# A GraphSAGE stack: edge rows of the late steps gathered by indirect DMA, layer-norm moments of three chunks on the scalar engine, the last chunk of the last layer in halves

## The chip, the cores and the metric

One core of one Trainium2 chip runs the whole program in one launch. The metric is the device time in microseconds. Engines are named PE (TensorE), DVE (VectorE), ACT (ScalarE), POOL (GpSimd) and SP (SyncE, which here only issues transfers).

## The reference

```python
h = maximum(layernorm(x), 0)          # x: 3125 x 256, no gain or bias
src, dst = edge_index                 # 50000 edges, sorted by dst
def sage(x, Wl, Wr, b):
    agg = segment_sum(x[src], dst)    # 3125 nodes
    deg = segment_sum(1, dst)
    return (agg / maximum(deg, 1)) @ Wl + x @ Wr + b
h = relu(sage(h, Wl1, Wr1, b1))       # 256 -> 256
h = relu(sage(h, Wl2, Wr2, b2))       # 256 -> 128
h = relu(sage(h, Wl3, Wr3, b3))       # 128 -> 256
out = x + sage(h, Wl4, Wr4, b4)       # 256 -> 256
```

## The kernel before

**The sum over edges as matmuls.** The kernel builds a dense matrix `counts` (source by destination, f16) and keeps it for all four layers. Destinations go in seven chunks: six of 512 (`CH`) and one of 53. They are worked in `ORDER = [5, 6, 4, 3, 2, 1, 0]`; "q=0" is the first of them, chunk 5. The aggregate of a chunk is, for each of 25 tiles k of sources (`NT`), four matmuls of 128x128 by 512 columns: two halves `h` of the features by two f16 `parts` (a high and a low part, `H[..., 0, :]` and `H[..., 1, :]`) of the features (`add_sources`, L1925). Then DVE scales by 1/degree (`scale_agg`, L1354), and PE applies the weights in f32 (`lin`: L1841 in layer 1, L1865 in layer 4).

**How counts is made.** Edges are cut into 892 "steps" of 128 edges, each for a window of four or eight destinations. Of each step DVE makes two one-hot tables with `is_equal` (`step`, L1261; a group of three or four steps in two instructions, three groups in flight), PE multiplies them into `window_ps` (L1776), and ACT copies each pair of windows, once done, into `counts` (L1546). `window_ps` has two banks, so PE is at most two pairs ahead of the copies. The steps are in `PIECES` of 64, 115, 358 and 355. The first 64 are made ahead of q=0 (call this stage -1), the next 115 (36 pairs of windows) inside q=0 from k=5 on, the others in q=2 to q=5. `script(q)` writes out the order of sums, steps and linear parts, and every engine follows the same script; `first_round`, at "sum k" of q=0, says what else DVE and ACT do at each k. The queues are in order, so an item in `first_round` delays everything behind it on its engine.

**The tables of the steps.** A step's 128 edges lie in the rows `src16` and `dst16` (98 partitions of 608 edges, row overlapping row). Where a step begins comes from the rank of its window (`lo`), by `bases`; `base_late` holds it in units of 32 edges. For pieces 2 and 3, `choose_late` (DVE, L1075) compares the bases with the number of each of 16 groups: 16 instructions of 98x358 for each piece. At k=13 and k=19 of q=0 (`SELECT_K`) PE fetches the edges with them: `select_rows` (L1707) is 16 matmuls for the sources and 16 for the destinations, each 98x128 by 358 columns. From the result ACT (`late_sources`, k=14 and 20; `spread_sources`, k=18 and 23) and DVE (`late_tables`, k=16 and 22) make `step_src` and `step_key`.

**Layer norm.** For place j of `ORDER`: `h0_moments(j)` on DVE (four `bn_stats`, L1014, four `bn_aggr`, L1017), `h0_root` on ACT (L1502), `h0_shift` on DVE, `h0_relu` on ACT (one instruction a tile, L1511), `h0_high_part` on ACT (L1518), `h0_low_part` on DVE (L1033). Moments of places 4, 5 and 6 are at k=1, 8 and 12 of q=0. PE's sums of q=0 go through the tiles in the order of the places: place 4's tiles from k=12, 5's from k=16, 6's from k=20.

**The end of layer 4.** Chunks alternate between the banks `agg_ps` and `window_ps`. The last chunk's 98 matmuls come with the linear part of the chunk before it at k=4; then two scalings (L1354), `lin(4, NCH - 1)` (16 f32 products, two records each, in groups of two tiles), two additions (`add_out`, L1456) and one store of 512 KB (L762).

## Time and profile before

| | us |
|---|---|
| median of 3 runs (lowest to highest) | 698.95 (697.97 to 699.79) |
| the profiled execution | 696.64 |
| its span | 694.9 |
| stage -1, ends about | 45.2 |
| q=0, from k=5 to its last sum | 58.3 to 107.6 |
| last chunk of layer 4, from its first matmul | 654.0 |

Busy time in the profiled execution: PE 647.0 us (93% of the span), DVE 307.6, ACT 170.1, POOL 33.3. An engine's busy time over the whole span is an average of very different stages: DVE is busy 90% of the time at first and hardly at all in the last layers. In the timeline each row merges instructions of a kind; its bracket is idle time of the engine just ahead and who ended it. A row of the table of stretches has the stretch, its length, the busy time (and number of instructions) of PE, PE's weight loads, DVE, ACT and POOL, the granted share of TensorE's full clock, the busy share of the DMA engines, and GB/s.

### The profile page before, as it was taken

Reading aid. Unit: us, or ns where it says so; the run is one execution under the profiler, and the core shown is the slowest. Engines: PE = TensorE matmul, PEld = TensorE weight load, DVE = VectorE, ACT = ScalarE, POOL = GpSimd, SP = SyncE. Lnnn points to the kernel's source line nnn. Section 1 sums busy time; section 2 is a strip of 40 time slices with the busy share of each in tenths; the row PEclk is TensorE's granted clock in tenths of the full one; section 3 lists DMA queues with packets and bytes.
Section 4 is the critical chain, followed back from the end, with each engine's and each line's share of the span. In section 5 each row is a group of like instructions: output and inputs, shape, how many; then the busy total and the mean of one; then the engine's idle time right before and its main releaser. Section 6 shows DMA issues by size and latency. Waiting matters only on the chain.

```text
span 694.9 us, 10754 instructions
## 1 busy us (share of the span) xinstructions
PE 647.0 (93%) x4179; PEld 350.3 (50%) x4180; DVE 307.6 (44%) x846; ACT 170.1 (24%) x335; POOL 33.3 (5%) x86
## 2 busy tenths in 40 slices
PE   5568898899999989999999999999999999999996
PEld 4234555665554545545444444544445646546554
DVE  6889876478897888932122222222221110101001
ACT  4844663264542631310011010211220000000000
POOL 7000000000000000000000000000001020110110
PEclk9999998899999999999999999999999999999999
DMA  8100020410100101013133122211131123032130
GB/s 253 42 3 3 15 81 2 173 36 5 44 22 20 62 18 64 1 21 125 57 130 108 60 75 92 64 65 61 60 98 69 38 80 107 1 106 63 43 106 31
DMA packets 33431, 43.49 MB, mean 63 GB/s; under 512 B 6031, under 2 KB 18851, under 8 KB 33385
## 3 DMA queue, kind: packets, MB, share of 16 engines
q1 hardware_dynamic: 33268, 42.62, 19.1%
q8 instruction: 31, 0.51, 0.3%
q10 hardware_dynamic: 116, 0.24, 0.1%
q14 instruction: 16, 0.12, 0.1%
HBM read 26.73 MB, written 15.79 MB: 61 GB/s over the span
## 4 chain that ended last, share of the span: by engine, by line
PE 84%; DVE 10%; ACT 3%; issue 2%; POOL 1%; DVEq 0%; POOLq 0%; ACTq 0%
PE agg_ps L1925 31%; PE window_ps L1925 21%; PE lin_ps L1841 7%; PE lin_ps L1865 6%; PE window_ps L1776 6%; PE lin_ps L1882 5%; DVE early L1261 4%; PE turn_ps L1907 2%; ACT counts L1546 1%; PE lin_ps L1890 1%; PE lin_ps L1947 1%; DVE rdeg L1339 1%; DVE aggT L1354 1%; PE degree_ps L1707 1%; PE turn_ps L1707 1%
## 5 line engine op out<-in xcount | busy, mean ns | idle before, releaser
L1925 PE MATMUL agg_ps<-counts,H 128*128 128x512 f16 (+3 forms) x1026 | 235.1, 355 | 5.9 <-DVE aggT L1354 5.9
L1261 DVE TENSOR_TENSOR early<-early 128x512 f16<-128x512 bf16 (+2 forms) x466 | 151.8, 390 | 26.1 <-PE window_ps L1776 25.0
L1546 ACT ACTIVATE counts<-window_ps 128x400 f16<-128x400 f32 x196 | 96.4, 504 | 127.1 <-PE window_ps L1776 123.2
L1776 PEld LDWEIGHTS window_ps<-early 128*128 128x128 f16 x892 | 68.8, 100 | 112.9 <-ACT counts L1546 31.8
L1776 PE MATMUL window_ps<-early 128*128 128x100 f16 (+1 forms) x892 | 100.5, 222 | 23.9 <-DVE early L1261 13.5
L1925 PEld LDWEIGHTS agg_ps<-counts,H 128*128 128x128 f16 (+1 forms) x1026 | 80.2, 98 | 61.3 <-issue 14.6
L1925 PE MATMUL window_ps<-counts,early 128*128 128x512 f16 (+2 forms) x396 | 89.0, 379 | 0.0
L1925 PE MATMUL window_ps<-counts,H 128*128 (+3 forms) x339 | 66.6, 351 | 0.0
L1925 PEld LDWEIGHTS window_ps<-counts,early 128*128 128x128 f16 (+1 forms) x396 | 38.4, 98 | 46.7 <-issue 3.4
L1925 PE MATMUL agg_ps<-counts,early 128*128 (+3 forms) x297 | 46.9, 314 | 0.0
L1925 PEld LDWEIGHTS window_ps<-counts,H 128*128 128x128 f16 (+1 forms) x339 | 29.4, 98 | 33.8 <-issue 1.5
L1354 DVE SCALAR_TENSOR_TENSOR aggT<-agg_ps,columns,rdeg 128x512 f32<-128x512 f32 (+1 forms) x27 | 17.0, 659 | 63.0 <-PE agg_ps L1925 56.6
L1354 DVE SCALAR_TENSOR_TENSOR aggT<-window_ps,columns,rdeg 128x512 f32<-128x512 f32 (+1 forms) x15 | 10.4, 716 | 67.1 <-PE window_ps L1925 64.7
L1587 ACT ACTIVATE newT<-lin_ps,columns 128x512 f32<-128x512 f32 (+1 forms) x28 | 17.3, 632 | 89.9 <-PE lin_ps L1882 57.3
L1362 DVE SCALAR_TENSOR_TENSOR partsT<-newT,columns,partsT 128x512 f16<-128x512 f32 (+1 forms) x21 | 14.4, 684 | 52.9 <-ACT partsT L1602 52.1
L1456 DVE TENSOR_TENSOR newT<-lin_ps,newH 128x512 f32<-128x512 f32 (+1 forms) x13 | 8.7, 671 | 58.3 <-PE lin_ps L1865 54.1
L943 POOL TENSOR_TENSOR newH<-newH,plan 128x256 f32<-128x256 f32 (+1 forms) x25 | 17.3, 723 | 356.7 <-DMA newH<-in_x_dram 356.7
L1925 PEld LDWEIGHTS agg_ps<-counts,early 128*128 128x128 f16 (+1 forms) x297 | 22.0, 97 | 23.8 <-issue 1.1
L1841 PE MATMUL lin_ps<-aggT,W 128*128 128x512 f32 (+1 forms) x56 | 27.6, 600 | 0.7 <-DVE aggT L1354 0.7
L1865 PE MATMUL lin_ps<-W,aggT 128*128 128x256 f32 (+1 forms) x100 | 25.8, 380 | 1.3 <-DVE aggT L1354 1.3
L1865 PE MATMUL lin_ps<-W,selfT 128*128 128x256 f32 (+1 forms) x100 | 25.7, 379 | 0.0
L1841 PE MATMUL lin_ps<-selfT,W 128*128 128x512 f32 (+1 forms) x56 | 25.6, 562 | 0.0
(185 smaller groups left out, 452.7 us busy)
## 6 DMA issues: line engine op xcount, KB each, us to landing
selfT<-hT_d SPq DMA_DIRECT2D x18, 512.0 KB, 4.3
hT_d<-newT SPq DMA_DIRECT2D x12, 512.0 KB, 4.3
rdeg<-rdeg_d SPq DMA_DIRECT2D x18, 256.0 KB, 4.3
counts<-in_x_dram SPq DMA_DIRECT2D x6, 512.0 KB, 8.0
hT_d<-counts SPq DMA_DIRECT2D x6, 512.0 KB, 3.2
newH<-in_x_dram SPq DMA_DIRECT2D x6, 512.0 KB
out_dram<-newT SPq DMA_DIRECT2D x6, 512.0 KB
hT_d<-newT SPq DMA_DIRECT2D x6, 256.0 KB, 4.0
```

What stands on the lines that cost most here:

```text
L943: nc.gpsimd.tensor_tensor(x4[0:q, i, :], x4[0:q, i, :], b4rows[0:q, :], ALU.add).then_inc(x4_biased, 1)
L1261: last = v.tensor_tensor(hot[:, group % GROUPS, 0:n * size].rearrange("p (r n d) -> p r n d", r=n, d=2), numbers_to[:, 0:size].rearrange(" ...
L1354: v.scalar_tensor_tensor(out=aggT[:, h, 0:n], in0=(agg_ps, window_ps)[bank][:, h, 0:n], scalar=unscale[:, l - 1:l], in1=rdeg[:, 0:n], op0= ...
L1362: v.scalar_tensor_tensor(out=low, in0=(lin_ps if l == 1 else newT)[:, h, 0:n], scalar=scale[:, l - 1:l], in1=partsT[:, 0, 0:n], op0=ALU.mu ...
L1546: a.activation(counts[:, :, 2 * w * WIN:2 * (w + 1) * WIN].rearrange("p t (a w) -> p a t w", a=2), window_ps[:, FILL_AT[w] % 2, 0:2 * KEYS ...
L1587: a.activation(newT[:, h, 0:n], source, ACT.Relu, bias=bT[:, bias + h:bias + h + 1]).then_inc(relu_done[l], 1)
L1707: last = m(ps, rows_[0:RP, g * FINE:g * FINE + P], picks[g][:, at:at + n], start=(g == 0), stop=(g == RG - 1))
L1776: m(window_ps[:, at % 2, key0:key0 + keys], hot_src[:, group % GROUPS, r * P:(r + 1) * P], hot_key[:, group % GROUPS, r * keys:(r + 1) * k ...
L1841: last = m(lin_ps[:, h, 0:n], W14[:, i // 2, i % 2, h * P:(h + 1) * P], (aggT, selfT)[i // 2][:, i % 2, 0:n], start=(i == 0), stop=(i == 3))
L1865: last = m(lin_ps[0:rows_, g, i * D:(i + 1) * D], h, w, start=(j == 0), stop=(j == len(ops) - 1))
L1882: last = m(lin_ps[:, h, 0:n], w, r, start=(i == 0), stop=(i == len(ops) - 1))
L1925: last = m((agg_ps, window_ps)[bank][:, h, 0:n], tile[:, part, h * P:(h + 1) * P], counts[0:rows_, k, chunk_cols(c, n)], start=first and p ...
```

## The change

- The rows of edges are written to DRAM (`rows_d`, 1568 rows of 256 f16: a destination part of 128 and a source part of 128, one row for each start in units of 32 edges) by eight transfers on SP's queue, behind the weight loads.
- `choose_late` goes (32 DVE instructions). `bases_late` at k=5 and 7 makes the bases; at k=8 (`BASES_K`) PE turns them into columns with six matmuls of 1x128 by 2; at k=10 DVE makes them integers (`late_rows`); POOL then issues six indirect transfers of up to 128 rows of 512 B. At k=13 and k=17 PE waits for three of these and makes six transposes in place of 32 matmuls (`turn_rows`). `late_sources(3)`, `spread_sources(3)` and `late_tables(3)` move to k=18, 21 and 20.
- Moments of places 4, 5 and 6 are made on ACT (`h0_moment`: two instructions with an accumulated output for each tile, each followed by a wait for itself). Place 4's four tiles lie behind windows 22, 24, 26 and 28 of stage -1, place 5's at k=1, 3, 5, 7, and place 6's at k=8, 9, 12, 13.
- Layer 4's last chunk is summed in two halves of 256 destinations in the two banks (`add_half`). The first half's scaling, eight linear products and two additions go between the second half's sums, and so do the other half's four products with `selfT`. Behind the last sum come two scalings of 256, four products, two additions, and the output goes tile by tile in four stores of 128 KB.
- `over_places` in layer 4 stops two places earlier; semaphores of layer 0 that nothing used are gone.

```diff
+            sp.wait_ge(rows_shifted, 2)
+            for at, rows_ in enumerate((dst16, src16)):
+                for b in range(SPAN):
+                    sp.dma_start(rows_d.rearrange("(p a b) (t e) -> p a b t e", a=RG // SPAN, b=SPAN, t=2)[:, :, b, at, :],
+                                 rows_[0:RP, b * FINE:b * FINE + REACH].rearrange("p (a e) -> p a e", e=P)
+                                 ).then_inc(rows_kept, 16)
...
+            pool.wait_ge(rows_kept, 16 * 2 * SPAN)
+            pool.wait_ge(first_rows_made, 1)
+            for i in range(2):
+                a, b = PIECES[2 + i]
+                for j in range(LATE_TILES):
+                    n = min(P, b - a - j * P)
+                    at = i * LATE_TILES + j
+                    g.indirect_dma_start(gathered_rows[i][j][0:n, :], None, rows_d[:, :],
+                                         bass.IndirectOffsetOnAxis(first_row[0:n, at:at + 1], 0)
+                                         ).then_inc(rows_gathered[i], 16)
...
-            first_round = {0: lambda: (h0_shift(3), below(), degrees(0)), 1: lambda: h0_moments(4),
-                           4: lambda: (h0_low_part(3), h0_shift(4)), 6: square_weights, 7: lambda: choose_late(2, 0),
-                           8: lambda: (h0_moments(5), h0_low_part(4)), 9: lambda: choose_late(2, 1),
-                           10: lambda: choose_late(2, 2), 11: lambda: (h0_shift(5), choose_late(2, 3)),
-                           12: lambda: h0_moments(6), 13: lambda: choose_late(3, 0),
-                           14: lambda: choose_late(3, 1), 15: lambda: (h0_low_part(5), h0_shift(6)),
-                           16: lambda: late_tables(2), 17: lambda: choose_late(3, 2),
-                           18: lambda: choose_late(3, 3), 19: lambda: h0_low_part(6), 22: lambda: late_tables(3)}
+            first_round = {0: lambda: (h0_shift(3), below(), degrees(0)), 4: lambda: (h0_low_part(3), h0_shift(4)), 6: square_weights, 5: lambda: bases_late(2), 7: lambda: bases_late(3),
+                           8: lambda: h0_low_part(4), 10: late_rows, 11: lambda: h0_shift(5),
+                           15: lambda: (h0_low_part(5), h0_shift(6)),
+                           16: lambda: late_tables(2), 19: lambda: h0_low_part(6), 20: lambda: late_tables(3)}
...
+            def h0_moment(j, i):
+
+                c = ORDER[j]
+                if i == 0:
+                    act.wait_ge(x_loaded[c], 16)
+                order.after(a.activation(spare, x_in[c][:, i, :], ACT.Copy, scale=-1.0 / D,
+                                         accum_out=moments[c][:, i, 0:1]))
+                ins = a.activation(spare, x_in[c][:, i, :], ACT.Square, bias=moments[c][:, i, 0:1],
+                                   accum_out=moments[c][:, i, 1:2])
+                order.after(ins)
...
+            def turn_rows(turn, piece):
+
+                a, b = PIECES[piece]
+                pe.wait_ge(rows_gathered[piece - 2], 16 * LATE_TILES)
+                for at, ps in zip((P, 0), table_ps(turn, b - a)):
+                    for j in range(LATE_TILES):
+                        n = min(P, b - a - j * P)
+                        last = nc.tensor.transpose(ps[:, j * P:j * P + n], gathered_rows[piece - 2][j][0:n, at:at + P],
+                                                   ident16[0:n, 0:n])
                 last.then_inc(steps_turned, 1)
...
+            bank = FIRST_BANK[4]
+            pe.wait_ge(agg_scaled[4], 2 * (NCH - 2))
+            for k in range(NT):
+                add_half(bank, k, 0)
+                if k == 8:
+                    lin(4, NCH - 2)
+            pe.wait_ge(agg_scaled[4], 2 * (NCH - 1))
+            for k in range(NT):
+                add_half(1 - bank, k, 1)
+                if k == 6:
+                    pe.wait_ge(self_loaded[4], 16 * NCH)
+                    pe.wait_ge(out_made, both(NCH - 1, 2, 1))
+                    for i in range(2):
+                        for j in range(2):
+                            last_lin(i, j, 1)
+                    pe.wait_ge(agg_scaled[4], 2 * NCH)
+                    for i in range(2):
+                        for j in range(2):
+                            last_lin(i, j, 0)
+                if k == 20:
+                    for i in range(2, 4):
+                        for j in range(2):
+                            last_lin(i, j, 1)
+            for j in range(2):
+                pe.wait_ge(agg_scaled[4], 2 * NCH + j + 1)
+                for i in range(2, 4):
+                    last_lin(i, j, 0)
```

## Rows read from the trace of the kernel before

**Rows 1.** The page: the chain that ended last, by engine.
```profile
PE 84%; DVE 10%; ACT 3%; issue 2%; POOL 1%; DVEq 0%; POOLq 0%; ACTq 0%
```
**Rows 2.** Busy time in stretches of stage -1, q=0 and q=1.
```profile
14.50:45.20 30.70, 16.30 (x72) 6.53 (x73) 26.71 (x95) 21.90 (x48) 0.20 (x1) 1.00 0.19 57
...
58.30:75.60 17.30, 13.44 (x97) 8.21 (x96) 16.55 (x71) 9.94 (x24) 0.00 (x0) 1.00 0.00 1
75.60:80.50 4.90, 4.90 (x35) 3.15 (x34) 3.05 (x12) 1.91 (x4) 0.00 (x0) 1.00 0.02 3
80.50:91.50 11.00, 9.38 (x79) 6.03 (x77) 10.19 (x30) 8.73 (x19) 0.00 (x0) 1.00 0.15 53
91.50:96.40 4.90, 4.90 (x37) 3.15 (x36) 1.67 (x5) 1.48 (x3) 0.00 (x0) 1.00 0.40 123
96.40:107.60 11.20, 9.35 (x66) 4.89 (x63) 7.88 (x22) 7.64 (x16) 0.00 (x0) 1.00 0.12 41
107.60:131.80 24.20, 20.40 (x188) 13.71 (x189) 13.51 (x41) 7.19 (x15) 0.00 (x0) 0.86 0.30 112
131.80:142.00 10.20, 9.92 (x143) 6.96 (x141) 5.99 (x20) 2.52 (x5) 0.00 (x0) 0.67 0.10 34
```
**Rows 3.** Timeline of PE: waits and selections in q=0, transposes in layer 3.
```profile
66.23 0.25 PE L1776 MATMUL window_ps<-early 128*128 128x100 f16 x2 [2.68 <-DVE early L1261]
...
75.64 2.61 PE L1707 MATMUL degree_ps<-counts 98*128 98x358 f16 x16
...
86.38 0.22 PE L1776 MATMUL window_ps<-early 128*128 128x100 f16 x1 [1.28 <-ACT counts L1546]
...
523.07 0.61 PE L1907 MATMUL turn_ps<-ident,partsT 128*128 128x128 f16 x8
```
**Rows 4.** Timeline of DVE in q=0.
```profile
61.03 0.98 DVE L1075 TENSOR_SCALAR counts<-counts 98x358 f16<-98x358 f16 x4
...
62.54 1.41 DVE L1014 BATCH_NORM_STATS2 counts<-counts 128x6 f32<-128x256 f32 x4
63.98 0.38 DVE L1017 BATCH_NORM_AGGREGATE counts<-counts 128x2 f32<-128x6 f32 x4
```
**Rows 5.** Timeline of ACT in stage -1, q=0 and q=1.
```profile
41.41 0.92 ACT L1546 ACTIVATE counts<-window_ps 128x400 f16<-128x400 f32 x2 [2.63 <-PE window_ps L1776]
42.52 0.50 ACT L1546 ACTIVATE counts<-window_ps 128x400 f16<-128x400 f32 x1 [0.19 <-PE window_ps L1776]
...
56.03 2.06 ACT L1511 ACTIVATE counts<-counts,newH 128x256 f32<-128x256 f32 x4
...
60.02 1.06 ACT L1518 ACTIVATE H<-counts 128x1024 f16<-128x1024 f32 x1
...
113.65 0.20 ACT L1538 ACTIVATE counts<-counts 128x1 f32<-128x1 f32 x1
```
**Rows 6.** DMA issues in the first 60 us: KB, us to landing.
```profile
columns<-in_L_gnn_b_dram SPq DMA_DIRECT2D x2, 1.0 KB, 3.0
```
**Rows 7.** Timeline of POOL at the start.
```profile
7.91 5.76 POOL L922 IOTA newT<- 128x128 f32 x15
```
**Rows 8.** Timeline of layer 4: its chunk of 53 columns, its last chunk.
```profile
537.33 1.37 PE L1925 MATMUL agg_ps<-counts,H 128*128 128x53 f16 x48
...
654.01 4.48 PE L1925 MATMUL window_ps<-counts,H 128*128 x20
...
682.06 1.41 DVE L1354 SCALAR_TENSOR_TENSOR aggT<-window_ps,columns,rdeg 128x512 f32<-128x512 f32 x2 [15.93 <-PE window_ps L1925]
683.52 1.13 PE L1865 MATMUL lin_ps<-W,aggT 128*128 128x256 f32 x4 [1.29 <-DVE aggT L1354]
...
690.73 0.69 DVE L1456 TENSOR_TENSOR newT<-lin_ps,newH 128x512 f32<-128x512 f32 x1 [2.66 <-PE lin_ps L1865]
691.50 0.39 SPq L762 DMA_DIRECT2D out_dram<-newT  x1
```
**Rows 9.** DMA while the last store moves.
```profile
692.50:693.00 0.50, 0.00 (x0) 0.00 (x0) 0.00 (x0) 0.00 (x0) 0.00 (x0) 1.00 1.02 350
```

More of the change, by code:

```diff
@@ L388, in sage_stack_kernel @@
         below_low = [row(17 + g // 4, g % 4 * 512, MID) for g in range(RG)]
-        chosen_late = [[row((21, 17)[i] + g // 5, g % 5 * LATE_N, LATE_N) for g in range(RG)] for i in range(2)]
+        gathered_rows = [[row(21 + i, 2 * P * j, 2 * P) for j in range(LATE_TILES)] for i in range(2)]
         bound_low = row(7, 0, MID)
@@ L471, in sage_stack_kernel @@
         steps_turned = sem("steps_turned")
+        rows_kept = sem("rows_kept")
+        bases_made = sem("bases_made")
+        bases_turned = sem("bases_turned")
+        first_rows_made = sem("first_rows_made")
+        rows_gathered = [sem(f"rows_gathered_{i}") for i in range(2)]
         src_whole = sem("src_whole")
@@ L539, in sage_stack_kernel @@
         x4_biased = sem("x4_biased")
+        last_products = [sem(f"last_products_{i}") for i in range(TPC)]
         out_made = sem("out_made")
+        rows_made = [sem(f"rows_made_{i}") for i in range(TPC)]
         out_stored = sem("out_stored")
+        last_stored = sem("last_stored")
         AGG = [0, 2, 1, 1, 2]
@@ L581, in sage_stack_kernel, with over_places @@
         FIRST_BANK = [0, 0, 1, 0, 1]
-        def over_places(eng, do, first):
+        def over_places(eng, do, first, places=NCH):
             do(1, 1 - first)
             do(2, first)
-            with eng.Fori(1, NCH // 2) as i:
+            with eng.Fori(1, (places - 1) // 2) as i:
                 do(2 * i + 1, 1 - first)
@@ L789, in after @@
                         double_tail(q + 1)
+                    if last and l == 4:
+                        for i in range(TPC):
+                            sp.wait_ge(rows_made[i], 1)
+                            c = ORDER[-1]
+                            sp.dma_start(out[c * CH + i * P:c * CH + (i + 1) * P, :],
+                                         newT[:, :, :].rearrange("p a b -> p (a b)")[:, i * D:(i + 1) * D]
+                                         ).then_inc(last_stored, 16)
+                        return
                     sp.wait_ge(lin_done[l], both(q + 1, LIN[l], 1 if l == 4 else LIN[l]))
@@ L1911, in turn, with add_half, last_lin @@
                 last.then_inc(turned[l], 1)
+            def add_half(bank, k, g):
+                cols = slice(g * HALF_CH, (g + 1) * HALF_CH)
+                c = ORDER[-1]
+                rows_, parts = (STACK, 1) if k == NT - 1 else (P, 2)
+                tile = H_tiles(4, k, 1)[0:rows_, 0, :, :]
+                for h in range(2):
+                    for part in range(parts):
+                        last = m((agg_ps, window_ps)[bank][:, h, cols], tile[:, part, h * P:(h + 1) * P],
+                                 counts[0:rows_, k, c * CH + g * HALF_CH:c * CH + (g + 1) * HALF_CH],
+                                 start=k == 0 and part == 0, stop=k == NT - 1)
+                    if k == NT - 1:
+                        last.then_inc(agg_done[4], 1)
+            def last_lin(i, k, of):
+                node = slice(i * P, (i + 1) * P)
+                m(last_ps(i), (aggT, selfT)[of][:, k, node], W14[:, of, k, :], start=of == 1 and k == 0,
+                  stop=of == 0 and k == 1).then_inc(last_products[i], 1)
             def add_sources(l, q, bank, k, first, final, halves=None):
```

140 lines of the change are left out of this document (94 added, 46 removed).

## The prediction

> **What bounds the kernel now.** I read the page first: the chain that ended last is PE for 84% of the span [rows 1], so from layer 2 on only PE's own work and the few places where it waits count. The change touches two stretches, and I read these alone: the first 108 us, by a table of stretches and the timelines of PE, DVE and ACT, and the last 41 us.
>
> In q=0 from k=5 on (58.3 to 107.6) no engine is the bound by itself [rows 2]. In 58.3:75.6 DVE is busy 16.55 of 17.3 us, PE 13.44, ACT 9.94, and PE's longest wait, 2.68 us, is for DVE's one-hot tables [rows 3]. In the two selections (75.6:80.5 and 91.5:96.4) PE is busy all of 4.9 us while DVE has 3.05 and 1.67 us of work and ACT 1.91 and 1.48 [rows 2]: there the time is PE's. Between them, in 80.5:91.5, DVE has 10.19, PE 9.38, ACT 8.73 of 11.0 [rows 2], with a wait of 1.28 us for ACT's copies [rows 3]. Over the five stretches from 58.3 to 107.6, PE has 42.0 us, DVE 39.3 and ACT 29.7. At the end PE stands still while DVE scales (1.41 us), then makes 16 products, and a last addition of 0.69 and a store follow [rows 8].
>
> **The selections.** 32 matmuls, two lots of the 16 that one row shows [rows 3], in 4.9 us [rows 2] become six transposes; eight of 128x128 issue within about 0.44 us (0.61 with the last one's own length) [rows 3], so 0.3 us. PE loses 4.6 us twice, 9.2 in all. The six small matmuls at k=8 are 0.3 us at most (a 53-column matmul issues each 26 ns: 48 in about 1.2 us [rows 8]). PE's work in q=0 falls from 42.0 to about 33.
>
> **DVE.** 32 comparisons at 0.98 us for four [rows 4] are 7.8 us; moments of places 5 and 6, 1.41 + 0.38 each [rows 4], 3.6 more (place 4's lie ahead of 58.3, where PE doesn't wait for them). The bases remain, and `late_rows` is one small instruction. DVE falls from 39.3 to 28.
>
> **ACT's new work.** No row shows an ACT instruction with an accumulated output. Of what rows show: 400 elements take 0.50 and 1024 take 1.06 [rows 5], so 0.9 ns an element, and the Copy of 256 is 0.37; the Square with its bias from memory is like the relu, 2.06 for four, 0.52 [rows 5]. To fetch an accumulator is at least nothing and perhaps a small instruction, 0.20 (the one-column root [rows 5]). A tile is thus 0.9 us below, 1.3 with two fetches, and, if each of the instructions also waits 0.1 for the one before, 1.7 above. I take 1.3: a value of one column has to be written by something. The chunk that cost DVE 1.8 us costs ACT 5.2.
>
> The Trainium skill, "ScalarE: Activation LUTs", Rules for kernel authors, speaks against such a move: simple arithmetic belongs on VectorE. By my rows the exchange is 5.4 us of DVE for 15.6 of ACT, which agrees, and by that rule alone this part would cost time; whether it does here depends on which engine the stretch waits for.
>
> **Stage -1** gets four tiles. ACT waits 2.63 us ahead of 41.41 [rows 5] while DVE plans, which takes in the tiles behind windows 24 and 26. The one behind 28 lies between the copy of 41.41 and that of 42.52, where PE waits for the copies, so 1.3 less the pauses there: about 0.5 us later. Bounds 0 and 2 us. Without DVE's pause at 39 the four would cost up to 5.2.
>
> **q=0 with ACT as the last to finish.** Ahead of k=5 place 5's tile at k=1 falls in idle time, but those of k=3 and k=5 stand around the relu that ends at 58.1 [rows 5], in front of the first copy of a window. So copies begin at 58.1 + 2.6 = 60.7. Up to k=13, ACT has its 9.94 [rows 2] and four more tiles, 5.2: 75.8 if it never waits. It waits for the squares at k=10, so 1 us more: 76.8, against 75.6 before. Here the change loses 1.2 us, though DVE and PE both have less to do. From there to k=20, ACT has 1.91 + 8.73 + 1.48 [rows 2] and one tile, 13.4; PE 0.3 + 9.38 + 0.3 and DVE 14.9 less half of the comparisons and more, about 10. With 1.5 us for pauses ACT comes to 91.7 where it was 96.4 before: 4.7 gained. The stretch 96.4:107.6 keeps its 11.2, since its table for piece 3 comes no later. Less the 0.5 of stage -1 this is 4.2 us. The bounds: tiles of 0.9 give 8 x 0.4 = 3.2 more (7.4); tiles of 1.7 give as much less (1.0).
>
> **The gathers.** The eight row stores stand on SP behind the weight loads, which run within the first 20 us; at the 3.0 us of a small transfer [rows 6] one after another they are done long before 60. The integer rows are made at k=10 of DVE, about 68 in the new run. POOL then issues three transfers, then three more. No row shows an indirect one: below, SP's 0.39 for 128 rows [rows 8]; above I have only POOL's general slowness. I take 1.2 us each, and 3.0 to land as a tiny load [rows 6]: 68 + 3.6 + 3 = 74.6, ahead of 76.8; the second three 78.2, ahead of k=17 at about 87. So nothing, with 2.2 us to spare: the first wait appears above 1.9 us each. Where they come late, PE waits at k=13 with the sums of q=0 and all windows behind it, and ACT and DVE run dry two or three windows later.
>
> The Trainium skill, "SBUF — State Buffer", section SBUF: two separate sides (its box, and the part A bandwidth-pool intuition that's wrong), states that GpSimd can't write descriptors while VectorE runs in a two-port mode, and that a transfer of 0.62 us then took 3.1. By that estimate the first three would be ready at 68 + 9.3 + 3 = 80.3, a wait of 3.5 us. The trace has 15 POOL instructions in 5.76 us, 0.38 each, beside a running DVE [rows 7], which doesn't show such a lock; those aren't descriptors, though.
>
> **The end.** The two halves cost no more than the whole: matmuls of 53 columns issue each 26 ns, so the weight loads don't bound 256 columns at 0.108 us; 196 of these are again 21.2. From 654.0 [rows 8] come 21.2, the 6.9 of the chunk before, and now 12 of the 16 products. Those took 7.2 us with all 16 (683.52 to about 690.7 [rows 8]), 0.43 each, so 5.2. The sums end at 687.3, instead of 682.1. Behind them: half a scaling, 0.45, then products of k=0 (0.86), whose cover is the second scaling, then k=1 (0.86), the last addition 0.4, some 0.1 for each hand-over: 2.9, so 690.2 where 691.4 stood. The store of 128 KB moves in 0.37 us where 512 KB took 1.5 at 350 GB/s [rows 9]; 1.0 more. Together 2.2. The waits between, for rdeg, x4 and the first half's scaling, are covered by six microseconds of second-half sums. Bounds: 1.0 (hand-overs of 0.3 each, and the stores' fixed time unchanged) and 2.8.
>
> **Sum.** 4.2 + 2.2 = 6.4 us. The profiled execution at 696.64 would become 690.2; it lies 2.3 below the median of the runs shown, so I put the same difference to the median: 698.95 - 6.4 = 692.6.
>
> **Rivals.**
> 1. ACT hides its new work: tiles near 0.9 us. For it: ACT is busy only 29.7 of 49.3 us. Against it: the tiles stand in front of copies that PE needs. q=0 gives 7.4, the end 2.2: 689.3.
> 2. ACT eats the gain: tiles of 1.7, stage -1 later by 2 us. q=0 then gives -0.5, only the end is left: 697.2.
> 3. The gathers come late, which ends slower. At 5 us each, 68 + 15 + 3 = 86, PE waits 9.2 at k=13; the second three at 101 against k=17 at 96, 5 more. 692.6 + 14.2 = 706.8. From about 4 us each it is slower than before (first wait 6.2, second 2.3: 701.1). For it: POOL has hardly worked beside DVE so far, and DVE is busy 16.55 of 17.3 us where the transfers are issued [rows 2]; against it: POOL's 15 instructions beside DVE [rows 7].
> 4. The clock. PE is granted full clock in all of q=0 and 0.86 and 0.67 of it in 107.6:131.8 and 131.8:142.0 [rows 2], after the thin work at the turn from q=0 to q=1. That is two spells at half speed, worth some 3 us each. The new run comes there 4 us earlier with the same thin work. A spell may go or come: 689.6 or 695.6, and within q=0, where PE is now busy less (about 70%), none is expected, since stage -1 kept full clock at 16.3 of 30.7 us [rows 2].
>
> **Chances.** The forecast, 690.5 to 695.5 with the clock as it was or one spell moved: 0.54. Rival 1: 0.16. Rival 2: 0.16. Rival 3: 0.14, of which a tenth still ends within 0.3%. 0.3% is 2.1 us, about what a measurement of this kernel can tell from no change, so 696.85 is where "faster" begins. Rival 2 lies on that line and gives 0.05 to faster, 0.09 to same, 0.02 to slower; the forecast gives 0.03 to same. Faster 0.72, same 0.13, slower 0.15. The range that leaves out 2 in 10 is 688 to 699.5: below it the best of rival 1, above it rival 3.
>
> **What would show it.** Right: in the new timeline of ACT pairs of instructions on 128x256 with a tile's four records at about 1.3 us; PE's waits in q=0 for ACT's copies, none over 0.3 us at k=13 and 17 for a DMA; k=13 near 77 and the turn to q=1 near 103; six transposes of 0.3 us; PE's last sums near 681 in that run (687.3 less what q=0 gave and then some 2.5 us to the last product). Wrong: a wait of PE behind a POOL transfer, tiles above 1.7 us, copies that start after 61, or a granted clock below 1.00 ahead of 100 us. What would upset the sum most is the pause of ACT I assumed (2.5 us in all), since no row shows ACT as the bound of this stage.

## The result, and the profile after

The changed kernel takes 691.42 us (median of four runs, 688.77 to 691.95), where before took 698.49 in the same job: 0.9894 of its time, interval 0.9866 to 0.9923. The forecast was 692.6, a gain of 6.4; it was 7.4 us by the ratio. The profiled execution took 688.77 us with a span of 687.0, 7.9 less than that of before. It is the fastest of its four, so its trace shows somewhat more gain than the medians (7.1 us).

The page of the changed kernel, chain that ended last (answers to [rows 1]) and its line for the windows' matmuls; below it the same line of the kernel before:

```profile
PE 83%; DVE 9%; ACT 4%; issue 2%; POOL 1%; DVEq 0%; POOLq 0%; ACTq 0%
...
L1885 PE MATMUL window_ps<-early 128*128 128x100 f16 (+1 forms) x892 | 100.8, 222 | 26.4 <-ACT counts L1630 13.0
```

```profile
L1776 PE MATMUL window_ps<-early 128*128 128x100 f16 (+1 forms) x892 | 100.5, 222 | 23.9 <-DVE early L1261 13.5
```

Of PE's idle time ahead of these matmuls (26.4 us, before 23.9) ACT now has the largest part, 13.0 us; before, DVE had it, 13.5. The stretches of [rows 2] in the changed kernel:

```profile
58.30:75.60 17.30, 14.92 (x100) 9.11 (x98) 12.43 (x44) 14.47 (x40) 5.28 (x6) 0.90 0.06 16
75.60:80.50 4.90, 2.32 (x20) 1.26 (x20) 2.44 (x7) 4.33 (x12) 0.80 (x1) 1.00 0.09 24
80.50:91.50 11.00, 8.27 (x71) 5.61 (x72) 8.88 (x23) 9.75 (x23) 0.00 (x0) 1.00 0.16 55
91.50:96.40 4.90, 4.01 (x32) 1.97 (x30) 4.83 (x14) 3.59 (x8) 0.00 (x0) 1.00 0.42 121
96.40:107.60 11.20, 8.21 (x79) 5.48 (x80) 6.08 (x17) 5.40 (x13) 0.00 (x0) 0.97 0.13 43
107.60:131.80 24.20, 21.83 (x256) 14.09 (x253) 13.78 (x46) 7.24 (x15) 0.00 (x0) 0.85 0.33 123
131.80:142.00 10.20, 10.20 (x85) 6.35 (x84) 7.11 (x22) 5.31 (x12) 0.00 (x0) 0.88 0.22 62
```

The fourth busy figure is ACT's: 14.47 of 17.3 where it had 9.94. DVE falls from 16.55 to 12.43. The granted clock of 58.3:75.6 is 0.90, where it was 1.00.

PE's timeline in q=0 of the changed kernel (answers to [rows 3]):

```profile
61.39 0.34 PE L1885 MATMUL window_ps<-early 128*128 128x200 f16 x2 [1.69 <-ACT counts L1630]
...
62.62 1.05 PE L2054 MATMUL agg_ps<-counts,H 128*128 128x512 f16 x2
...
76.64 0.22 PE L1885 MATMUL window_ps<-early 128*128 128x100 f16 x1 [1.49 <-issue]
...
77.21 0.32 PE L1816 MATMUL degree_ps<-ident,counts 128*128 128x128 f16 x3
77.37 0.32 PE L1816 MATMUL turn_ps<-ident,counts 128*128 128x128 f16 x3
77.53 0.59 PE L2054 MATMUL agg_ps<-counts,H 128*128 128x512 f16 x2
...
79.18 0.26 PE L1885 MATMUL window_ps<-early 128*128 128x100 f16 x2 [1.01 <-ACT counts L1630]
...
81.87 0.22 PE L1885 MATMUL window_ps<-early 128*128 128x100 f16 x1 [1.91 <-ACT counts L1630]
```

Six transposes take 0.32 us, from 77.21 to the next sum at 77.53, in place of 4.9. The waits behind them are for ACT. The one just ahead, 1.49 us at 76.64, the trace puts down to issue (see "Open" below). The pair of sums at 62.62 takes 1.05 instead of 0.59: a spell at half clock, which the kernel before didn't have there.

ACT and POOL (answers to [rows 5] and [rows 7]): one tile of moments, the first copies, three of the gathers.

```profile
48.75 0.40 ACT L1575 ACTIVATE counts<-counts 128x256 f16<-128x256 f32 x1
49.06 0.19 ACT L1575 ACTIVATION_READ_ACCUMULATOR counts<-counts 128x1 f32 x1
49.28 0.51 ACT L1577 ACTIVATE counts<-counts 128x256 f16<-128x256 f32 x1
49.69 0.19 ACT L1577 ACTIVATION_READ_ACCUMULATOR counts<-counts 128x1 f32 x1
...
60.83 1.44 ACT L1630 ACTIVATE counts<-window_ps 128x400 f16<-128x400 f32 x3
```

```profile
68.80 1.15 POOL L975 DMA_INDIRECT counts<-edge_rows,counts  x1 [54.25 <-DVE counts L1127]
70.25 0.94 POOL L975 DMA_INDIRECT counts<-edge_rows,counts  x1 [0.30 <-issue]
71.50 1.09 POOL L975 DMA_INDIRECT counts<-edge_rows,counts  x1 [0.30 <-issue]
```

A tile is 48.75 to 49.88, 1.13 us. The six gathers start 1.25 to 1.45 us apart (68.80 to 75.42).

The end (answers to [rows 8]), PE, DVE and SP:

```profile
648.16 4.09 PE L2030 MATMUL window_ps<-counts,H 128*128 128x256 f16 x36
...
681.75 0.88 DVE L1537 SCALAR_TENSOR_TENSOR aggT<-agg_ps,columns,rdeg 128x256 f32<-128x256 f32 x2 [8.84 <-PE agg_ps L2030]
682.29 0.70 PE L2039 MATMUL degree_ps<-W,aggT 128*128 128x256 f32 x2 [0.47 <-DVE aggT L1537]
...
684.32 0.42 DVE L1544 TENSOR_TENSOR newT<-turn_ps,newH 128x256 f32<-128x256 f32 x1
684.34 0.81 SPq L824 DMA_DIRECT2D out_dram<-newT  x2
```

From the last chunk's first matmul to the end of the span it is 38.8 us (648.16 to 687.0), where it was 40.9 (654.01 to 694.9).

### The profile page after: what moved, and what is told of

The parts are those of the page before. It is cut to its first block, busy times and chain, and to the rows that moved or that the text cites. A ratio compares the mean times of both kernels' runs of the same rounds, so it can differ in the third digit from the quotient of the medians.

```text
span 687.0 us, 10750 instructions
## 1 busy us (share of the span) xinstructions
PE 638.7 (93%) x4231; PEld 353.5 (51%) x4232; DVE 296.7 (43%) x795; ACT 182.1 (27%) x383; POOL 39.2 (6%) x91
## 4 chain that ended last, share of the span: by engine, by line
PE 83%; DVE 9%; ACT 4%; issue 2%; POOL 1%; DVEq 0%; POOLq 0%; ACTq 0%
PE agg_ps L2054 31%; PE window_ps L2054 18%; PE lin_ps L1950 7%; PE window_ps L1885 6%; PE lin_ps L1974 5%; PE lin_ps L1991 5%; DVE early L1311 4%; ACT counts L1630 2%; PE turn_ps L2016 2%; PE window_ps L2030 2%; PE agg_ps L2030 2%; PE lin_ps L1999 1%; PE lin_ps L2076 1%; DVE rdeg L1389 1%; DVE aggT L1404 1%
## 5 line engine op out<-in xcount | busy, mean ns | idle before, releaser
L1311 DVE TENSOR_TENSOR early<-early 128x512 f16<-128x512 bf16 (+2 forms) x466 | 151.6, 387 | 27.2 <-PE window_ps L1885 25.8
L1885 PE MATMUL window_ps<-early 128*128 128x100 f16 (+1 forms) x892 | 100.8, 222 | 26.4 <-ACT counts L1630 13.0
L2054 PE MATMUL window_ps<-counts,early 128*128 128x512 f16 (+2 forms) x346 | 78.0, 379 | 0.0
L2054 PE MATMUL window_ps<-counts,H 128*128 128x512 f16 (+2 forms) x291 | 55.9, 346 | 0.0
L2054 PEld LDWEIGHTS window_ps<-counts,early 128*128 128x128 f16 (+1 forms) x346 | 33.5, 98 | 40.9 <-issue 3.4
L2054 PE MATMUL agg_ps<-counts,early 128*128 (+4 forms) x297 | 46.9, 314 | 0.0
L1671 ACT ACTIVATE newT<-lin_ps,columns 128x512 f32<-128x512 f32 (+1 forms) x28 | 17.3, 632 | 89.9 <-PE lin_ps L1991 57.3
L2054 PEld LDWEIGHTS window_ps<-counts,H 128*128 128x128 f16 x291 | 24.7, 97 | 28.3 <-issue 1.5
L992 POOL TENSOR_TENSOR newH<-newH,plan 128x256 f32<-128x256 f32 (+1 forms) x25 | 17.3, 724 | 358.2 <-DMA newH<-in_x_dram 358.2
L1404 DVE SCALAR_TENSOR_TENSOR aggT<-window_ps,columns,rdeg 128x512 f32<-128x512 f32 (+1 forms) x13 | 9.0, 711 | 50.9 <-PE window_ps L2054 48.9
L1502 DVE TENSOR_TENSOR newT<-lin_ps,newH 128x512 f32<-128x512 f32 (+1 forms) x11 | 7.3, 667 | 51.3 <-PE lin_ps L1974 51.3
L1671 ACT ACTIVATE newT<-newT,columns 128x512 f32<-128x512 f32 (+1 forms) x7 | 4.7, 667 | 69.6 <-DVE newT L1516 69.6
L1974 PE MATMUL lin_ps<-W,aggT 128*128 128x256 f32 (+1 forms) x84 | 21.6, 380 | 0.0
```

The costliest lines, as they stand in the source:

```text
L992: nc.gpsimd.tensor_tensor(x4[0:q, i, :], x4[0:q, i, :], b4rows[0:q, :], ALU.add).then_inc(x4_biased, 1)
L1311: last = v.tensor_tensor(hot[:, group % GROUPS, 0:n * size].rearrange("p (r n d) -> p r n d", r=n, d=2), numbers_to[:, 0:size].rearrange(" ...
L1404: v.scalar_tensor_tensor(out=aggT[:, h, 0:n], in0=(agg_ps, window_ps)[bank][:, h, 0:n], scalar=unscale[:, l - 1:l], in1=rdeg[:, 0:n], op0= ...
L1671: a.activation(newT[:, h, 0:n], source, ACT.Relu, bias=bT[:, bias + h:bias + h + 1]).then_inc(relu_done[l], 1)
L1885: m(window_ps[:, at % 2, key0:key0 + keys], hot_src[:, group % GROUPS, r * P:(r + 1) * P], hot_key[:, group % GROUPS, r * keys:(r + 1) * k ...
L1974: last = m(lin_ps[0:rows_, g, i * D:(i + 1) * D], h, w, start=(j == 0), stop=(j == len(ops) - 1))
```

## The experiments

All ratios are against the kernel before, run in the same job. The medians of that kernel in the three jobs are 698.76 (first four rows), 698.92 (next four) and 698.46 (last four).

| kernel | median us | ratio, interval |
|---|---|---|
| halves alone | 696.56 | 0.9975, 0.9959 to 0.9991 |
| moments alone | 696.52 | 0.9964, 0.9949 to 0.9979 |
| gathers and moments, last chunk whole | 692.49 | 0.9918, 0.9897 to 0.9938 |
| gathers alone | 691.29 | 0.9893, 0.9875 to 0.9912 |
| gathers threefold | 704.98 | 1.0092, 1.0067 to 1.0118 |
| five tiles early | 690.27 | 0.9870, 0.9837 to 0.9904 |
| gathers and halves | 688.37 | 0.9854, 0.9827 to 0.9881 |
| place 5 on ACT | 686.02 | 0.9823, 0.9794 to 0.9851 |
| changed kernel again | 690.86 | 0.9893, 0.9862 to 0.9923 |
| gathers and halves again | 688.29 | 0.9860, 0.9831 to 0.9890 |
| place 5 on ACT again | 686.02 | 0.9836, 0.9806 to 0.9865 |
| waits filled | 687.06 | 0.9851, 0.9821 to 0.9880 |

**Halves alone.** The kernel before with `add_half`, `last_lin`, the tile-by-tile additions and stores, the shorter `over_places` and the unused semaphores gone, and nothing else of the change:

```diff
-                over_places(pe, place, FIRST_BANK[l])
-            lin(4, NCH - 1)
+                if l < 4:
+                    over_places(pe, place, FIRST_BANK[l])
+            over_places(pe, place, FIRST_BANK[4], NCH - 2)
+            place(NCH - 2, 0 if FIRST_BANK[4] else 1)
...
```

> The kernel before with the last chunk of layer 4 in halves and nothing else. Theory A (the end gives its own 2 us, apart from the rest): 2.1 us less than before, about 696.4, with the same time from the last chunk's first matmul to the end of the span as the changed kernel has (38.8 us, where before has 40.9). Theory B (the end's gain hangs on what comes ahead, or is noise of the profile): no difference, 698.5.

1.7 us less by the ratio (0.25% of 698.8), 2.2 by the medians. The trace gives the size apart from what the rest of the run does:

```profile
654.31 1.41 DVE L1372 SCALAR_TENSOR_TENSOR aggT<-agg_ps,columns,rdeg 128x512 f32<-128x512 f32 x2 [16.03 <-PE agg_ps L1989]
```

The scaling of the chunk ahead starts at 654.31 and the span ends at 693.1, which is 38.8 us. In the kernel before it is 654.00 to 694.9, 40.9 us, so the end is 2.1 us shorter. Theory A.

**The changed kernel with the last chunk whole.** The same edit the other way round:

```diff
-            over_places(pe, place, FIRST_BANK[4], NCH - 2)
-            place(NCH - 2, 0 if FIRST_BANK[4] else 1)
...
+                over_places(pe, place, FIRST_BANK[l])
+            lin(4, NCH - 1)
```

> The changed kernel with the last chunk whole, as before. Theory A: gathers and moments together give 4.5 us in q=0 and about 1 us in the clock, so 693.0 to 693.5. Theory B: all of the 7 us, 691.5.

0.9918 is 5.7 us, a little more than the 5.5 of theory A; the median, 692.49, lies between the two theories, and the interval (4.3 to 7.2 us) takes in both. With the 1.7 us of the halves 5.7 makes the 7.4 of the whole change, so the end and the rest add up as far as these intervals can tell.

**Gathers alone.** From the one before, the moments go back to DVE, and ACT's twelve tiles go:

```diff
-        ON_ACT = 4
+        ON_ACT = NCH
...
-            first_round = {0: lambda: (h0_shift(3), below(), degrees(0)), 4: ...
+            first_round = {0: lambda: (h0_shift(3), below(), degrees(0)), 1: lambda: h0_moments(4), 4: ...
-                           8: lambda: h0_low_part(4), 10: late_rows, 11: lambda: h0_shift(5),
+                           8: lambda: (h0_moments(5), h0_low_part(4)), 10: late_rows, 11: lambda: h0_shift(5),
+                           12: lambda: h0_moments(6),
```

> Gathers alone: moments stay on DVE, the last chunk whole. Theory A (ACT with its 24 new instructions is what q=0 waits for in the changed kernel, and DVE's relief by the comparisons is enough): more gain than with the moments on ACT, 7 to 9 us, 690 to 691.5, and PE's waits for ACT near 3 us instead of 7.5. Theory B (DVE bounds q=0 as long as it has the moments): 3 to 4 us, 694.5 to 695.5, with waits of PE for DVE as in the kernel before.

7.5 us, as much as the whole change gives, without the halves. So theory A in its main point, though its margin over gathers and moments (1.2 us by the medians) is small and the intervals overlap. That PE's waits for ACT would fall to 3 us was wrong, and those for DVE stay large:

```profile
PE window_ps L1840 <- DVE early L1294: 6.7, 5, 2.6
PE window_ps L1840 <- ACT counts L1588: 5.2, 7, 1.4
```

(engine and tile that waited in 40:105 of the profiled execution, what for, us in total, times, longest; in the changed kernel 7.5 for ACT and 3.6 for DVE, in gathers and moments 6.3 and 3.6).

**Moments alone.** The kernel before with the four edits of the change that concern moments:

```diff
+        ON_ACT = 4
...
-                           8: lambda: (h0_moments(5), h0_low_part(4)), 9: ...
+                           8: lambda: h0_low_part(4), 9: ...
-                           12: lambda: h0_moments(6), 13: ...
+                           13: ...
```

and ACT's tiles where the change has them.

> Moments of three chunks on ACT alone: comparisons and selections as before, the last chunk whole. Theory A (ACT's order in front of the first window copies costs about what DVE's relief gives): within 1.5 us of before, 697 to 700. Theory B (DVE is the bound and its relief pays by itself): 3 us faster, 695.5.

2.5 us less by the ratio (2.2 by the medians), between the theories and nearer to B. The trace doesn't show this gain in q=0. From the end of stage -1 to ACT's copy of the degrees (`rdeg`) it takes 60.9 us (45.97 to 106.84), before 61.0 (45.22 to 106.20). What differs is the granted clock of the executions: 0.989 to 0.990 in the six of this kernel (695.3 to 697.2 us), where eleven of the eighteen of before in the same job have 0.986 or 0.987 (698.4 to 699.8 us). The four of before at 0.989 take 696.4 to 697.4 us, as this kernel does. So the gain goes with the clock, and whether the move brings that about isn't shown. What the trace does show is why the tiles cost nothing. With the selections in place, ACT has time to work off its copies while PE selects:

```profile
75.60:80.50 4.90, 4.80 (x33) 3.06 (x34) 1.99 (x8) 4.76 (x14) 0.00 (x0) 1.00 0.00 0
```

ACT, which had 1.91 us of work there before [rows 2], has 4.76, under PE's 4.80. With the gathers this cover is gone. By the ratios the parts alone sum to 7.5 + 2.5 + 1.7 = 11.7 us, and together they give 7.4.

**Gathers threefold.** The changed kernel with

```diff
+                    more = [row(18 + i, 2 * P * (2 * j + r), 2 * P) for r in range(2)]
+                    for into in more + [gathered_rows[i][j]]:
+                        g.indirect_dma_start(into[0:n, :], None, rows_d[:, :],
...
-                pe.wait_ge(rows_gathered[piece - 2], 16 * LATE_TILES)
+                pe.wait_ge(rows_gathered[piece - 2], 16 * 3 * LATE_TILES)
```

> The changed kernel with each gather issued three times, twice into cells that nothing reads, and PE waits for all. One takes 1.27 us from issue to issue in the changed kernel, so the first nine are in at about 68.8 + 11.4 + 1.5 = 81.7 where PE asks at 77.2. Theory A (slack of the first three about 4 us, and once they are late PE's wait is partly paid back, since ACT works off its copies meanwhile): PE waits 4.5 us at k=13, the run takes 2 to 3 us more, 693.5. Theory B (the forecast's rival as it was worked out, nothing paid back): 4.5 and 1 us more at k=17, 696.9. Theory C (transfers from POOL are held up by DVE): still later, over 700.

14 us slower than the changed kernel. At over 700 it is where theory C put it, but not for that reason:

```profile
75.36 1.03 POOL L977 DMA_INDIRECT counts<-edge_rows,counts  x1 [0.30 <-issue]
78.48 1.10 POOL L977 DMA_INDIRECT counts<-edge_rows,counts  x1 [2.09 <-issue]
...
81.30 1.08 POOL L977 DMA_INDIRECT counts<-edge_rows,counts  x1 [0.30 <-issue]
```

```profile
90.22 0.94 POOL L977 DMA_INDIRECT counts<-edge_rows,counts  x1 [0.30 <-issue]
```

```profile
75.58 0.22 PE L1887 MATMUL window_ps<-early 128*128 128x100 f16 x1 [0.46 <-ACT counts L1632]
...
84.29 0.46 PE L1818 MATMUL degree_ps<-ident,counts 128*128 128x128 f16 x3 [7.97 <-DMA counts<-edge_rows,counts]
...
98.71 0.46 PE L1818 MATMUL degree_ps<-ident,counts 128*128 128x128 f16 x3 [4.31 <-DMA counts<-edge_rows,counts]
```

```profile
82.00:84.00 2.00, 0.00 (x0) 0.00 (x0) 0.00 (x0) 0.00 (x0) 1.35 (x2) 0.50 0.15 40
...
86.00:88.00 2.00, 2.00 (x12) 1.44 (x11) 1.95 (x5) 1.30 (x3) 1.70 (x2) 0.50 0.22 66
```

Seventeen of the eighteen gathers take 0.94 to 1.16 us. The one at 90.22 takes 0.94 with DVE busy all the time, and those at 79.89 and 81.30 take 1.10 and 1.08 with DVE idle. One, at 87.20, takes 1.47, with DVE busy for 1.44 of it. So DVE isn't what makes them late. But POOL stands idle for 2.09 us ahead of the seventh, where it is 0.30 between the first six (and 1.02 and 2.07 later); why, the trace doesn't say. PE waits 7.97 and 4.31 us, and in the wait its clock falls to half and stays there when work is back. In sum nothing is paid back: ACT's copy of the degrees comes 12.1 us later than in the changed kernel (113.75 against 101.66), with 12.3 us of these waits. The ninth gather ends at 82.38 and PE goes on at 84.29, so a gather lands 1.9 us after POOL is done with it. By that, the third of the changed kernel, which ends at 72.59, is there at an estimated 74.5, and PE asks at 77.2: 2.7 us to spare.

**Five tiles early.** The changed kernel with

```diff
-            first_round = {0: lambda: h0_whole(3), 1: lambda: h0_moment(5, 0), 2: lambda: (h0_root(4), first_rows(3, ...)),
-                           3: lambda: h0_moment(5, 1), 4: lambda: h0_relu(4, (0, 1)),
-                           5: lambda: (h0_relu(4, (2, 3)), h0_moment(5, 2)), 6: lambda: h0_high_part(4),
-                           7: lambda: h0_moment(5, 3), 8: lambda: h0_moment(6, 0),
+            first_round = {0: lambda: h0_whole(3),
+                           1: lambda: (h0_moment(5, 0), h0_root(4), h0_moment(5, 1), h0_moment(5, 2), h0_moment(5, 3),
+                                       h0_moment(6, 0)),
+                           2: lambda: first_rows(3, ...),
+                           4: lambda: h0_relu(4, (0, 1)), 5: lambda: h0_relu(4, (2, 3)), 6: lambda: h0_high_part(4),
```

> The changed kernel with five of ACT's tiles (all of place 5 and the first of place 6) at k=1, in the 5.7 us in which ACT waits for the ranks, and no longer in front of the first copies and between later ones. Theory A (what costs is where the tiles stand: two of 1.13 us in front of the first copy): PE's wait of 1.69 us at 61.4 goes, k=13 comes 2 us earlier, 688.5 to 689.5. Theory B (ACT's total bounds the stretch, wherever the tiles stand): it had idle time for these five, so the same 2 to 3 us, but waits for ACT stay over 7 us. Theory C: DVE takes over as the bound: no change, 691.

690.27, about 1 us under the changed kernel, not shown apart from it. The wait of 1.69 us for ACT did go, and one for DVE stands in its place, 0.2 us shorter:

```profile
62.40 0.25 PE L1885 MATMUL window_ps<-early 128*128 128x200 f16 x1 [1.48 <-DVE early L1311]
```

DVE squares the weights at k=6, 2.6 us of work, which I take to be what it waits behind. So mainly theory C, for this wait. k=13 comes at 76.68, 0.5 us earlier and not 2. The waits for ACT behind it are as they were (1.00 and 1.91 us). In its profile, q=0 also holds 10.2 us at half clock, which hides what the rest of the move gave.

**Gathers and halves, twice.** The changed kernel with the edit of gathers alone.

> The changed kernel with the moments of places 4, 5 and 6 back on DVE (at k=1, 8 and 12): gathers and halves. Gathers alone measured 691.3 and halves alone took 0.25% off. Theory A (with the gathers in place the move of moments to ACT costs time, since PE then waits for ACT's copies): faster than the changed kernel, 689.4. Theory B (the difference between gathers alone and gathers with moments was chance, in the clock's half-speed spells): as the changed kernel, 691.

> Gathers and halves, moments on DVE, again. Theory A (moments on ACT cost time once the gathers are in): 1.5 to 3 us below the changed kernel of this call. Theory B (chance): within 1 us of it.

**The changed kernel again**, in the job of the second one.

> The changed kernel once more, so that it shares a chip and the runs of before with the next three. Both theories: 691, ratio near 0.989.

688.29 against 690.86 in one job, and 688.37 against 691.42 in two. The ratios' intervals overlap (0.9831 to 0.9890 and 0.9862 to 0.9923), but both are against the same executions of before. Execution by execution the changed kernel is the slower in 33 of the 36 pairs of that job, and at the same granted clock of 0.988 it takes 689.3 to 691.4 us against 688.6 to 689.1. Gathers alone and the same with moments differ the same way in another job. So I take it that the move costs 1 to 3 us once the gathers are in.

**Place 5 on ACT, twice.** From gathers and halves:

```diff
-        ON_ACT = NCH
+        ON_ACT = 5
...
-                           8: lambda: (h0_moments(5), h0_low_part(4)), 10: late_rows, 11: lambda: h0_shift(5),
+                           8: lambda: h0_low_part(4), 10: late_rows, 11: lambda: h0_shift(5),
...
-            first_round = {0: lambda: h0_whole(3), 2: ...
+            first_round = {0: lambda: h0_whole(3), 1: lambda: [h0_moment(5, i) for i in range(TPC)], 2: ...
```

and the three tests for `j < ON_ACT` become `j != ON_ACT` (DVE's and ACT's waits on `moments_made` leave out place 5's).

> Gathers and halves with the moments of place 5 alone on ACT, all four tiles at k=1 while it waits for the ranks; places 4 and 6 on DVE at k=1 and 12, where DVE has nothing else to do. Theory A (each engine's free time takes what fits): DVE's pause ahead of k=8 (PE waited 1.52 us there in gathers alone) goes and ACT's copies are untouched, 688. Theory B (PE or the clock bounds q=0 by now): as gathers and halves, 689.4.

> Place 5's moments on ACT at k=1, the rest on DVE, again. Theory A: 686, 4 to 5 us below the changed kernel and 2 below gathers and halves. Theory B: as gathers and halves.

686.02 in both, by the medians 12.4 to 12.9 us under before, 4.8 under the changed kernel of the same job and 2.3 under gathers and halves: theory A, and 2 us more than it said at first (688). Paired execution by execution with gathers and halves of the same job, it is the faster in 60 of 61 pairs. It is the fastest version here. ACT, second run:

```profile
53.18 0.19 ACT L1578 ACTIVATION_READ_ACCUMULATOR counts<-counts 128x1 f32 x1
53.40 0.30 ACT L1587 ACTIVATE newH<-counts 128x4 f32<-128x4 f32 x1
56.05 0.69 ACT L1706 ACTIVATE counts<-degree_ps,counts 128x512 f16<-128x512 f32 x1 [2.36 <-PE degree_ps L1785]
```

All four tiles are done by 53.37, and ACT still waits 2.36 us for the ranks. PE's wait for DVE behind the six small matmuls of k=8 (1.52 us in gathers alone, 1.63 and 2.29 in the two runs of gathers and halves) is gone.

**Where the moved tiles cost, by the traces.** Each row is one profiled execution. The two stretches are from the end of stage -1 to k=13 (the selection or the first transpose), and from there to ACT's copy of the degrees, with the time at half clock in each.

| kernel | to k=13, at half clock | behind k=13, at half clock |
|---|---|---|
| before | 30.4, 0 | 30.6, 0 |
| moments alone | 30.3, 0 | 30.6, 0 |
| changed kernel | 31.6, 3.4 | 24.5, 0 |
| changed kernel again | 32.1, 3.4 | 25.8, 3.4 |
| gathers and moments | 31.6, 3.4 | 25.0, 3.4 |
| five tiles early | 31.1, 3.4 | 26.2, 6.8 |
| gathers alone | 35.0, 6.8 | 22.1, 0 |
| gathers and halves | 36.1, 6.8 | 22.1, 0 |
| gathers and halves again | 32.6, 3.4 | 22.1, 0 |
| place 5 on ACT | 31.9, 0 | 22.1, 0 |
| place 5 on ACT again | 31.2, 3.4 | 22.1, 0 |
| waits filled (below) | 32.9, 0 | 22.1, 0 |

Behind k=13 it is 22.1 us in all six traces in which DVE makes place 6's moments, and 24.5 or more in the four with the gathers in which ACT makes them. The changed kernel's first trace ran that stretch at full clock (24.45 us against 22.12), so 2.3 us is the price of place 6's tiles behind k=12 and k=13, in front of copies that PE waits for. With the selections in place they cost nothing there (30.6 in both). Ahead of k=13, ACT's tiles rather save: 31.1 to 32.1 us, where gathers with all moments on DVE take 32.6 to 36.1. Place 5 on ACT keeps that and pays nothing behind k=13. In the changed kernel PE waits 1.91 us for ACT at 81.87; in gathers and halves again, at the same place:

```profile
80.45 0.22 PE L1883 MATMUL window_ps<-early 128*128 128x100 f16 x1 [0.74 <-ACT counts L1631]
```

**Waits filled.** Gathers and halves with

```diff
+                    if q == 0 and k in (6, 8):
+                        for i in range(6 if k == 6 else 8):
+                            m(turn_bank[:, :], H[:, TILES[0], 0, 0:P], counts[:, TILES[0], chunk_cols(ORDER[0], CH)],
+                              start=True, stop=True)
```

> Gathers and halves with 14 idle-time matmuls of 128x128 by 512 into a bank that nothing reads, six at k=6 and eight at k=8 of q=0, where PE waited 1.42 and 2.29 us for DVE. They add 3.0 us of work to PE inside 3.7 us of waits. Theory A (PE's waits there are what brings the half-speed spell in q=0, worth 1.6 us for 3.4 us of it): no half clock in q=0 and 1.5 to 3 us less than gathers and halves, about 686. Theory B (the spells have another cause): the same time or up to 1 us more.

1.2 us less than gathers and halves of the same job, short of the 1.5 that theory A asked for. The same stretch, first gathers and halves again, then this one's fillers:

```profile
62.00:64.00 2.00, 1.48 (x9) 0.85 (x10) 2.00 (x14) 0.61 (x2) 0.00 (x0) 0.77 0.00 0
64.00:66.00 2.00, 2.00 (x10) 0.94 (x8) 1.86 (x8) 0.90 (x2) 0.00 (x0) 0.50 0.00 0
```

```profile
59.98 1.46 PE L2165 MATMUL turn_ps<-counts,H 128*128 128x512 f16 x6
61.28 0.59 PE L2052 MATMUL agg_ps<-counts,H 128*128 128x512 f16 x2
...
65.63 1.90 PE L2165 MATMUL turn_ps<-counts,H 128*128 128x512 f16 x8
```

With the fillers the granted clock stays at full until 104. The granted clocks of the six executions point the same way: 0.990 to 0.995, against 0.988 to 0.990 in gathers and halves (one at 0.975). That is for theory A's cause, though of the nine traces without fillers one has no spell in q=0 either. It is not for its saving. In this trace q=0 is no shorter than in gathers and halves again (32.9 and 22.1 us against 32.6 and 22.1); the trace gains behind q=0, where the half-speed spell is 3.4 us instead of 6.8. The size in the medians is within what the intervals leave open.

## Why the prediction was right, and where it wasn't

**By its own steps.** The times are of the two profiled executions. The forecast's points in q=0 leave out the 0.5 us of stage -1, which its sum takes off at the end.

| step | forecast | measured |
|---|---|---|
| a tile of moments on ACT | 1.3 us | 1.13 us |
| stage -1 later by | 0.5 us | 0.36 us (45.22 to 45.58) |
| first copy of a window | 60.7 | 60.83 |
| k=13 | 76.8 | 77.21 |
| the sum that started at 96.40 before | 91.7 | 91.65 |
| six transposes | 0.3 us | 0.32 us |
| a gather; first three there | 1.2 us; 74.6 | 1.3 us from start to start; an estimated 74.5 |
| q=0 ends earlier by (ACT's copy of the degrees) | 4.2 us | 4.5 us (106.20 to 101.66) |
| last sum to last addition | 2.9 us | 3.0 us (681.75 to 684.74) |
| the end shorter by | 2.2 us | 2.1 us |
| clock at the turn to q=1 | as before, or 3 us either way | 1.3 us less |

The two terms came out as they were worked out, the end by experiment too: the halves gave 2.1 us of the trace by themselves. The 7.9 us of the traces are 4.5 + 1.3 + 2.1. The 1.3 is what lies between q=0's end and layer 4's last chunk (which starts 5.85 us earlier); the granted clock there points to the half-speed spell after q=0, which is 3.4 us long where it was 6.8. No run moved that spell alone. But over all fourteen traces the stretch from ACT's copy of the degrees to that chunk's first scaling takes 547.7 to 548.3 us in the six whose spell behind q=0 is 6.8 us, and 545.8 to 546.9 in the eight where it is 3.4. The shorter spell came in eight of the ten traces with the six gathers and in none of the others.

**The size was right; of the two reasons in q=0 one held.** The one that held is the selections: they go, and behind k=13 PE then waits for ACT, as forecast. That stretch was to become 5.9 us shorter (76.8 to 91.7, where it was 75.6 to 96.4) and became 6.3 shorter (77.21 to 91.65).

The other is the loss up to k=13. The forecast put 1.2 us there, and 0.5 for stage -1, because ACT would be the last to finish. The trace has 1.6 us, but the agreement is in good part luck. The threefold run is the same kernel up to k=13. Its PE gets there at 76.32 (84.29 less the wait of 7.97), 30.5 us behind the end of its stage -1, where before took 30.4. So on their way to k=13 the tiles of q=0 cost about 0.1 us, as in moments alone: the wait for ACT at 61.39 takes the place of one for DVE (2.68 us at 66.23 [rows 3]). What the changed kernel's profiled execution has lost over that run, 0.9 us, is close to what its wait at 76.64 is longer (1.49 against 0.46 us), and that wait isn't explained.

**What wasn't worked out.** With the gathers in, only the price of ACT's tiles was asked for and not whether the move should be there at all. Gathers and halves without it are 2.6 us faster in one job, and with only the four tiles that fit into ACT's wait for the ranks, 4.8 us.

**Its sums.** Two slips change nothing in the forecast. The bounds of q=0 take 8 tiles at 0.4 us, though the one at k=1 was said to fall in idle time; with 7 they are 7.0 and 1.4 us and not 7.4 and 1.0. And at 4 us a gather the second wait by the prediction's own numbers is 1.8 us (95 against 93.2), not 2.3.

The Trainium skill, "ScalarE: Activation LUTs", Rules for kernel authors, which the prediction weighed, puts simple arithmetic on VectorE. The trace agrees on the price: 1.13 us a tile on ACT against 0.45 on DVE. It agrees on the outcome only behind k=13 with the gathers in (2.3 us lost). With the selections in place the tiles cost nothing, and four of them at k=1 go with the fastest version.

**Wrong: within q=0 no half-speed spell was expected.** The argument was that stage -1 keeps full clock at 53% busy. It didn't carry over. Of the ten traces with the six gathers eight show a spell of 3.4 us or more between 62 and 92; that with filled waits and one of the two of place 5 show none, and neither does any of the three traces without gathers. In the changed kernel 62.6 to 65.7 holds three pairs of sums with their windows at 1.1 us each instead of 0.57, so 1.6 us more work, 1.1 us behind the end of PE's wait of 1.69. That this wait brings it is supported by the filled waits, but not settled. The same wait of 1.69 us is followed by no spell in moments alone and in the threefold run, and neither is that of 2.68 us in the kernel before. Nor did the spell cost 1.6 us: the threefold run, at full clock, waits 0.40 us for ACT and 0.60 for DVE in that stretch instead, and both come to the products behind it at the same time (67.39 and 67.35).

**The rival with late gathers, tested.** It took PE's wait as the whole price. The threefold run makes a gather cost 4.5 us (three in 68.77 to 82.38). By the rival's rule that gives waits of 7.8 and 3.4 us and 703.8 us; measured are 7.97 and 4.31, and 704.98. So the rule was good to about 1 us, with POOL's pauses counted in the 4.5. The side that mattered, that six gathers arrive in time, was right, with 2.7 us to spare against 2.2 (1.8 where PE is as early as in the threefold run).

The Trainium skill, "SBUF — State Buffer", section SBUF: two separate sides, would have each transfer at about 3.1 us beside a DVE in two-port mode. No run here shows such a lock: the gathers took 0.94 to 1.15 us in the changed kernel. Its DVE was busy only 2.9 of the 8 us from 68 to 76, so this alone would say little. But the gather at 90.22 in the threefold run took 0.94 us and the one at 75.90 in gathers alone 1.10, with DVE busy all the time of each. Whether these DVE instructions run in such a mode no run tells.

**Open.** PE's wait of 1.49 us at 76.6 in the changed kernel, which the trace puts down to issue; ACT's copy at 76.08, which may be what it waited for, itself waited 0.58 us for PE. Gathers and moments has the same wait (1.51 us). The second trace of the changed kernel has 0.46 us for ACT in its place, and it isn't in the traces of gathers and halves or of place 5.

## What to carry to other kernels

When one part of a change takes the bound off an engine, price the other parts again without it: the tiles that moved from DVE to ACT cost nothing while PE's selections covered them, and 2.3 us behind k=13 once the selections were gone. Where moved work stands in the queue counts as much as how long it is: four tiles in the 5.7 us that ACT waits anyway were free, and those of place 6, in front of copies that PE needs, were not. A stretch that comes out as forecast can still do so for another reason, so compare it in a second run that is the same up to there. And before a difference of 2 us in the medians is put down to a wait, look at the granted clock of the executions and at whether the trace has it.

## What the runs showed that was not expected

- An ACT instruction with an accumulated output has a second row, ACTIVATION_READ_ACCUMULATOR, 0.19 us each.
- POOL's indirect transfers of up to 128 rows follow each other at 1.3 us up to the sixth; ahead of the seventh POOL stood idle for 2.09 us instead of 0.30. Where PE waited for them, they had landed 1.8 to 1.9 us after POOL was done.
- TensorE's clock fell to half behind waits of PE of 1.4 to 2.3 us inside q=0, for 3.4 or 6.8 us, and in a wait of 7.97 us it fell before the work came back. But a wait of 2.68 us in the kernel before brought no spell, and the same kernel's spells differ between executions: the two traces of place 5 have one at 63 to 66 us or none in q=0.
- The device time goes with the granted clock of the execution. The kernel before takes 698.4 to 700.4 us at 0.986 or 0.987, 696.4 to 697.4 at 0.989 and 694.7 to 695.3 at 0.993 or 0.995; one execution at 0.972, which took 698.3, doesn't fit.
- Halving a sum's columns from 512 to 256 cost nothing: 36 matmuls from 648.16 to 652.09, 0.109 us each, behind 39 of 512 columns from 639.74, 0.216 each.
